# A graph network's last pass: how its row sums and squared deviations are made

## The chip, the cores and the metric

The kernel runs on one core of one Trainium2 chip. A core has TensorE (matrix products), VectorE, ScalarE (functions of one input), GpSimd (general cores, which also issue the indirect transfers), SyncE (which issues plain transfers) and 16 DMA engines between the HBM and its on-chip memory (SBUF, with 128 partitions; TensorE writes to a smaller one, PSUM). The metric is the device time of one execution in microseconds.

## The reference, cut to what matters

Eight layers of a graph network run over 10000 nodes with 512 features and 10000 edges; then the input is added and every row is normalised:

```
for W, b, g, beta in layers:                       # 8
    h = h * norm_out
    agg = segment_sum(h[src], dst) * norm_in
    h = gelu(layer_norm(agg @ W + b, g, beta))
y = x + h
out = (y - mean(y)) / sqrt(var(y) + 1e-5)          # row by row, 512 columns
```

The last two lines are the pass that the change touches.

## The kernel before, in words

After a setup that sorts edges and destinations, each layer gathers rows, sums them with TensorE, multiplies by the layer's weights and normalises. Nodes that receive edges are kept as packed rows; the layer's rows are stored to an HBM table, `h_rows`, and the index `idx_f` says which of its rows belongs to which node.

The last pass goes over 79 tiles of 128 nodes (the last one has 16). The tiles of the input x lie already in `agg_t`, SBUF that the layers no longer need; SyncE loads them beside the last layer. Each engine has its own program, in order, and the engines meet only at semaphores:

- GpSimd issues one indirect transfer per tile (`gather`, L526), which brings the 128 rows of `h_rows` into one of `FS` = 8 row buffers. A gather waits until the addition eight tiles earlier has freed the buffer.
- VectorE adds the buffer onto the tile in place (`add`, L961), takes the batch statistics of the 512 columns (`spread`, L965) and sums them up to mean and variance (`mean`, L969). It runs one addition ahead of the statistics.
- The rest goes by groups of tiles: 1, 1, 2, then groups of 4 (`GROUPS`, 22 in all, the last one of 3). ScalarE adds epsilon to a group's variances (`add_eps`, L1101), GpSimd raises them to the power -1/2 (L537), VectorE makes the shift, minus mean times that (`shift`, L974), and ScalarE scales and shifts each tile in place (`result`, L1107).
- SyncE stores each finished tile (L414).

The order written into the programs matters. GpSimd first issues eight gathers; then, for each group q, it issues the gathers of the tiles eight ahead of it (in the steady part those of group q+2) and behind them the power of group q. VectorE's shift of a group comes `LATE` = 4 tiles after its end (2 for the first groups); the last two shifts come at the very end. ScalarE's order is the epsilon of group q, then the scaling of group q-1. The variances, means and shifts have places for 16 tiles.

Of the kernel before, what the change touches and what calls it, by code (L numbers as in the profile page):

```python
# [6 lines left out]
D = 512  # L7
LAYERS = 8
EPS = 1e-5
P = 128  # L10
# [8 lines left out]
FS = 8  # L19
LATE = 4  # L20
# [16 lines left out]
ALU = mybir.AluOpType  # L37
ACT = mybir.ActivationFunctionType
# [22 lines left out]
def build(nc, x, src, dst, dst_prev, dst_row, Ws, bs, ln_g, ln_b, out):  # L61
# [3 lines left out]
    with ctx:  # L65
# [3 lines left out]
        def sem(n):  # L69
            return ctx.enter_context(nc.semaphore(n))  # L70
# [8 lines left out]
        with nc.sbuf_tensor("rows", [P, UN, D], f32) as gathered:  # L79
            rows = gathered  # L80
# [28 lines left out]
        ps_y = [ctx.enter_context(nc.psum_tensor(f"ps_y{i}", [P, D], f32)) for i in range(2)]  # L109
        ps_z = ctx.enter_context(nc.psum_tensor("ps_z", [P, D], f32))  # L110
        ps_l = [ps_g[:, 2 * i:2 * i + 2, :, :].rearrange("p a k n -> p (a k n)") for i in range(2)]
        ps_f = [ps_g[:, i, :, :].rearrange("p k n -> p (k n)") for i in range(GS)]
# [7 lines left out]
        def view(flat, shape, d):  # L120
            if d is not f32:
                flat = flat.bitcast(d)
            if len(shape) == 3:
                flat = flat.rearrange("p (a b) -> p a b", b=shape[2])
            if len(shape) == 4:
                flat = flat.rearrange("p (a b c) -> p a b c", b=shape[2], c=shape[3])
            if len(shape) == 5:
                flat = flat.rearrange("p (a b c d) -> p a b c d", b=shape[2], c=shape[3], d=shape[4])
            return flat

        def words(shape, d):
            size = 1
            for n in shape[1:]:
                size *= n
            return size * (2 if d is bf16 else 4) // 4

        def part(shape, d=f32):
            n = words(shape, d)
            flat = agg_t[:, :, :].rearrange("p k n -> p (k n)")[0:shape[0], Space.at:Space.at + n]
            Space.at += n  # L140
            return view(flat, shape, d)
# [82 lines left out]

        GX = 4
        Space.at = (GX - 1) * PADDED + (NR // GX - 1) * D
        f_stats, f_mean = part([P, FS, 6]), part([P, 2 * FS, 2])
        f_var, f_rstd, f_shift = part([P, 2 * FS]), part([P, 2 * FS]), part([P, 2 * FS])
        assert GX == KB and Space.at <= KB * PADDED

        def final_rows(t, n):

            at = t // GX * D
            return agg_t[0:n, t % GX, at:at + D]
# [67 lines left out]
        x_in = sem("x_rows_in")  # L302
        hf_in = [sem(f"h_tile_in{k}") for k in range(FS)]
        f_sum = sem("residual_added")
        f_st = sem("final_stats")
        f_mv = sem("final_mean_var")
        f_ve = sem("final_var_eps")
        f_rs = sem("final_rstd")
        f_sh = sem("final_shift")
# [21 lines left out]
        FULL = N // P  # L331
        TAIL = N - FULL * P
        QUADS = NR // GX
        TILES = [(t, P if t < FULL else TAIL) for t in range(FULL + 1)]
        ENDS = [1, 2, 4] + list(range(GX + GX, FULL - 2, GX)) + [FULL - 2, FULL + 1]
        GROUPS = list(zip([0] + ENDS[:-1], ENDS))

        def places(g):

            first = GROUPS[g][0] % (2 * FS)  # L340
            return slice(first, first + GROUPS[g][1] - GROUPS[g][0])
# [200 lines left out]
        def _(dve):  # L542
            v = nc.vector
# [33 lines left out]
            for n, high, low in ((2, dst_hi, dst_lo), (0, src_hi, src_lo)):  # L577
                for c in range(NE // HT):
                    own, packs = slice(c * HT, c * HT + HT), slice(c * HT // G, (c + 1) * HT // G)
# [181 lines left out]
            for c in range(CH):  # L761
                k = c % 2
                if c >= 2:
                    dve.wait_ge(put_ok, c - 1)
                own = slice(c * CT, c * CT + CT)
# [192 lines left out]
            def add(t, n):  # L958
                dve.wait_ge(hf_in[t % FS], 16 * (t // FS + 1))
                own = final_rows(t, n)  # L960
                v.tensor_tensor(own, own, rows[0:n, t % FS, :], ALU.add).then_inc(f_sum, 1)  # L961

            def spread(t, n):
                dve.wait_ge(f_sum, t + 1)
                v.bn_stats(f_stats[0:n, t % FS, :], final_rows(t, n)).then_inc(f_st, 1)  # L965

            def mean(t, n):
                dve.wait_ge(f_st, t + 1)
                v.bn_aggr(f_mean[0:n, t % (2 * FS), :], f_stats[0:n, t % FS, :]).then_inc(f_mv, 1)  # L969

            def shift(q):
                own = places(q)
                dve.wait_ge(f_rs, q + 1)
                v.scalar_tensor_tensor(f_shift[:, own], f_mean[:, own, 0], -1.0, f_rstd[:, own],  # L974
                                       ALU.mult, ALU.mult).then_inc(f_sh, 1)

            dve.wait_ge(x_in, 16 * (QUADS - 1 + FULL % GX + 1))
            add(*TILES[0])
            for t, n in TILES:
                if t < FULL:  # L980
                    add(*TILES[t + 1])
                if t > 0:
                    mean(*TILES[t - 1])
                spread(t, n)
                for q, end in enumerate(ENDS[:-2]):
                    if t == end + (LATE if end > GX else LATE // 2):
                        shift(q)
            mean(*TILES[FULL])
            shift(len(GROUPS) - 2)
            shift(len(GROUPS) - 1)  # L990


        @block.scalar
        def _(act):
            a = nc.scalar
# [27 lines left out]
            for lev in range(LEVELS + 1):  # L1023
                first, end = lev * CH, lev * CH + CH
# [70 lines left out]
                w_stage(L, pairs, its, pb, ib)  # L1095


            def add_eps(q):
                own = places(q)
                act.wait_ge(f_mv, GROUPS[q][1])  # L1100
                a.activation(f_var[:, own], f_mean[:, own, 1], ACT.Copy, bias=EPS).then_inc(f_ve, 1)  # L1101

            def result(q):
                act.wait_ge(f_sh, q + 1)
                for t, n in TILES[GROUPS[q][0]:GROUPS[q][1]]:
                    k, own = t % (2 * FS), final_rows(t, n)
                    a.activation(own, own, ACT.Identity, bias=f_shift[0:n, k:k + 1], scale=f_rstd[0:n, k:k + 1])\  # L1107
                     .then_inc(f_o, 1)

            for q in range(len(GROUPS)):  # L1110
                add_eps(q)
                if q > 0:
                    result(q - 1)
            result(len(GROUPS) - 1)
# [216 lines left out]
```

## Time and profile before

| What | Value |
|---|---|
| median of 3 runs | 1397.96 us (1397.11 to 1398.72) |
| the profiled execution: its span | 1400.9 us |
| the profiled execution: its own time | shown by its span alone, 1400.9 us |
| busy TensorE / VectorE / ScalarE / GpSimd | 1057.1 / 909.9 / 518.2 / 845.7 us |
| the last pass: first gather to the end of the span | 1255.6 to 1400.9 us |
| DMA in the last pass | 41.01 MB, mean 281 GB/s |
| out stores, landing (median) | 4.1 us |

Times in the trace are microseconds from the start of the span. A line such as L526 is a line of the kernel. The profiled execution is one of its own, so a difference is worked out within it and then laid on the median of the runs. An engine's gap is put down to what released it; "issue" is a gap in which it waited for nothing that the profile shows.

### The profile page before, as it was taken

Reading aid. Unit: us, or ns where it says so; the run is one execution under the profiler, and the core shown is the slowest. Engines: PE = TensorE matmul, PEld = TensorE weight load, DVE = VectorE, ACT = ScalarE, POOL = GpSimd, SP = SyncE. Lnnn points to the kernel's source line nnn. Section 1 sums busy time; section 2 is a strip of 40 time slices with the busy share of each in tenths; the row PEclk is TensorE's granted clock in tenths of the full one; section 3 lists DMA queues with packets and bytes.
Section 4 is the critical chain, followed back from the end, with each engine's and each line's share of the span. In section 5 each row is a group of like instructions: output and inputs, shape, how many; then the busy total and the mean of one; then the engine's idle time right before and its main releaser. Section 6 shows DMA issues by size and latency. Waiting matters only on the chain.

```text
span 1400.9 us, 29723 instructions
## 1 busy us (share of the span) xinstructions
PE 1057.1 (75%) x6307; PEld 863.9 (62%) x6307; DVE 909.9 (65%) x2155; ACT 518.2 (37%) x842; POOL 845.7 (60%) x1025
## 2 busy tenths in 40 slices
PE   7896695886968968959968977899688899960000
PEld 7673244776757857857857866788577778840000
DVE  7787895574674764755754774477644377757876
ACT  5324302333324324333334333433244434422545
POOL 1577204566556655655666657667577566658885
PEclk9885597998989989989989999999899999985555
DMA  9700004526336245264265226622466694557998
GB/s 347 270 5 4 2 0 133 153 98 190 119 121 194 85 155 166 82 182 126 90 184 178 85 102 195 186 91 90 142 197 202 183 365 177 176 175 245 322 305 288
DMA packets 98031, 224.47 MB, mean 160 GB/s; under 512 B 14496, under 2 KB 14496, under 8 KB 97968
## 3 DMA queue, kind: packets, MB, share of 16 engines
q0 software_dynamic: 34432, 104.72, 25.7%
q1 hardware_dynamic: 57104, 107.19, 21.4%
q10 hardware_dynamic: 6432, 11.86, 2.3%
q8 instruction: 21, 0.34, 0.1%
q14 instruction: 42, 0.34, 0.1%
HBM read 137.91 MB, written 85.82 MB: 160 GB/s over the span
## 4 chain that ended last, share of the span: by engine, by line
PE 49%; DMA 12%; issue 11%; POOL 9%; DVEq 8%; DVE 8%; ACT 3%; POOLq 0%; ACTq 0%; SPq 0%
PE ps_y L1289 10%; PE ps_y L1294 10%; PE ps_y L1290 10%; DMA rows<-h_rows,slot 7%; PE ps_a L1260 6%; DVEq L863 5%; POOL rows L526 5%; DMA h_rows<-rows 3%; PE ps_y L1285 2%; PE ps_a L1175 2%; PE ps_y L1194 2%; POOL rows L471 2%; PE ps_a L1241 1%; POOL agg_t L537 1%; DMA rows<-h_rows,idx_f 1%
## 5 line engine op out<-in xcount | busy, mean ns | idle before, releaser
L1260 PE MATMUL ps_a<-sel,rows 128*128 128x128 f32 x2560 | 364.3, 293 | 147.4 <-DMA rows<-h_rows,slot 123.2
L1260 PEld LDWEIGHTS ps_a<-sel,rows 128*128 128x128 f32 x2560 | 324.9, 201 | 188.4 <-issue 184.8
L471 POOL DMA_INDIRECT rows<-h_rows,slot x290 | 278.1, 959 | 136.7 <-issue 77.2
L485 POOL TENSOR_TENSOR s_lo<-agg_t,s_hi 128x512 fp32r<-128x512 f32 x168 | 216.9, 1293 | 189.9 <-ACT s_hi L1060 189.9
L1055 ACT ACTIVATE agg_t<-ps_a 128x508 f32 x320 | 190.7, 596 | 348.1 <-PE ps_a L1260 340.9
L830 DVE TENSOR_SCALAR sel<-iota,by_tile 128x128 f32<-128x128 f32 x344 | 136.4, 400 | 227.2 <-issue 227.2
L1289 PE MATMUL ps_y<-w_hi,s_hi 128*128 128x512 f32 x672 | 262.6, 391 | 3.2 <-ACT s_hi L1060 2.8
L1290 PE MATMUL ps_y<-w_lo,s_hi 128*128 128x512 f32 x672 | 261.6, 389 | 0.0
L1294 PE MATMUL ps_y<-w_hi,s_lo 128*128 128x512 f32 x672 | 179.6, 389 | 0.0
L914 DVE BATCH_NORM_STATS2 small<-ps_y 128x6 f32<-128x512 f32 x168 | 117.2, 698 | 63.2 <-PE ps_y L1294 62.4
L1289 PEld LDWEIGHTS ps_y<-w_hi,s_hi 128*128 128x128 f32 x672 | 126.1, 188 | 33.6 <-issue 7.7
L1294 PEld LDWEIGHTS ps_y<-w_hi,s_lo 128*128 128x128 f32 x672 | 126.1, 188 | 26.3
L1290 PEld LDWEIGHTS ps_y<-w_lo,s_hi 128*128 128x128 f32 x672 | 126.1, 188 | 25.8
L1060 ACT ACTIVATE s_hi<-agg_t 128x512 fp32r (+1 forms) x168 | 104.8, 628 | 89.5 <-PE ps_y L1294 42.1
L455 POOL DMA_INDIRECT rows<-out_degrees,agg_t x80 | 79.5, 994 | 62.4 <-DVE agg_t L626 43.2
L493 POOL TENSOR_TENSOR small<-small 128x1 f32<-128x1 f32 x168 | 95.3, 567 | 14.0
L526 POOL DMA_INDIRECT rows<-h_rows,idx_f x79 | 84.1, 1064 | 29.4 <-issue 21.4
L1065 ACT ACTIVATE rows<-ps_a 128x512 f32<-128x512 f32 x84 | 50.3, 599 | 133.6 <-DVE ps_a L929 126.4
L1065 ACT ACTIVATE rows<-ps_z 128x512 f32<-128x512 f32 x84 | 50.4, 600 | 124.9 <-DVE ps_z L929 113.5
L471 POOL DMA_INDIRECT rows<-in_x,slot x30 | 28.8, 958 | 84.2 <-issue 82.0
L961 DVE TENSOR_TENSOR agg_t<-agg_t,rows 128x512 f32<-128x512 f32 (+1 forms) x79 | 54.1, 685 | 32.3 <-DMA rows<-h_rows,idx_f 31.8
L921 DVE SCALAR_TENSOR_TENSOR ps_z<-ps_y,small,rows 128x512 f32<-128x512 f32 x84 | 63.7, 759 | 16.4 <-ACT rows L1065 5.6
(212 smaller groups left out, 1286.5 us busy)
## 6 DMA issues: line engine op xcount, KB each, us to landing
h_rows<-rows SPq DMA_DIRECT2D x124, 256.0 KB, 2.0
h_rows<-agg_t SPq DMA_DIRECT2D x1, 20480.0 KB, 58.6
out<-agg_t SPq DMA_DIRECT2D x78, 256.0 KB, 4.1
agg_t<-in_x SPq DMA_DIRECT2D x19, 1024.0 KB, 5.9
h_rows<-rows ACTq DMA_DIRECT2D x44, 256.0 KB, 2.3
w_raw<-in_Ws SPq DMA_DIRECT2D x32, 256.0 KB, 2.9
rows<-h_rows,slot POOLq DMA_INDIRECT x290, 3.7
rows<-in_ln_g SPq DMA_DIRECT2D x8, 256.0 KB, 3.7
```

Source lines behind the costliest of these rows:

```text
L471: g.indirect_dma_start(out=rows[:, k, :], out_offset=None, in_=table[:, :], in_offset=bass.IndirectOffsetOnAxis(ap=slot[:, k:k + 1], axis=0))\
L485: g.tensor_tensor(s_lo[:, k, :, :], agg_t[:, :, bass.ds(c * P, P)], s_hi[:, k, :, :].bitcast(f32), ALU.subtract).then_inc(lo_ok, 1)
L526: g.indirect_dma_start(out=rows[0:n, t % FS, :], out_offset=None, in_=hbuf[:, :], in_offset=bass.IndirectOffsetOnAxis(ap=idx_f[0:n, t:t + ...
L830: v.tensor_scalar(sel[:, k % GS, :], iota[:, :], rel[:, bass.ds(i, 1)], wgt[:, bass.ds(i, 1)], ALU.is_equal, ALU.mult).then_inc(sel_ok, 1)
L914: v.bn_stats(stats[:, k, :], ps_y[k][:, :]).then_inc(st_ok, 1)
L1055: a.activation(agg_t[:, :, bass.ds(r0 + 1, P - 1)], ps_a[k % GS][:, :, 1:P], ACT.Copy)\
L1060: a.activation(s_hi[:, k, :, :], agg_t[:, :, bass.ds(c * P, P)], ACT.Copy).then_inc(hi_ok, 1)
L1065: a.activation(made[k], ps_t[k], ACT.Gelu).then_inc(h_ok, 1)
L1260: m = mm(ps_a[k % GS][:, b, :], rows[:, k, b * P:(b + 1) * P], sel[:, k % GS, :], start=True, stop=True)
L1289: mm(ps_y[k][:, :], s_hi[:, k, b, :], w_hi[:, b, :], start=False, stop=False)
L1290: mm(ps_y[k][:, :], s_hi[:, k, b, :], w_lo[:, b, :], start=False, stop=False)
L1294: m = mm(ps_y[k][:, :], s_lo[:, k, b, :], w_hi[:, b, :], start=False, stop=b == KB - 1)
```

## The change: row sums from the addition, squares from ScalarE

The addition also gives the sum of each row. VectorE turns a group's sums into negated means. ScalarE computes the square of each tile with that negated mean as bias, writes the squares to PSUM (they are not used again) and keeps their sum; VectorE turns a group's sums into variance plus epsilon. The batch statistics and ScalarE's epsilon go. VectorE's program now goes by groups: the additions of group q, with the variance of group q-2 behind the first of them, then the mean of q and the shift of q-2. ScalarE's order is the squares of q, then the scaling of q-1. GpSimd's program is as it was.

```diff
             def add(t, n):
                 dve.wait_ge(hf_in[t % FS], 16 * (t // FS + 1))
                 own = final_rows(t, n)
-                v.tensor_tensor(own, own, rows[0:n, t % FS, :], ALU.add).then_inc(f_sum, 1)
+                v.scalar_tensor_tensor(own, own, 1.0, rows[0:n, t % FS, :], ALU.mult, ALU.add,
+                                       accum_out=f_total[0:n, t % (2 * FS):t % (2 * FS) + 1]).then_inc(f_sum, 1)
+
+            def mean(q):
+                own = places(q)
+                dve.wait_ge(f_sum, GROUPS[q][1])
+                v.tensor_scalar(f_negm[:, own], f_total[:, own], -1.0 / D, None, ALU.mult).then_inc(f_nm, 1)
+
+            def variance(q):
+                own = places(q)
+                dve.wait_ge(f_sq, GROUPS[q][1])
+                v.tensor_scalar(f_var[:, own], f_square[:, own], 1.0 / D, EPS, ALU.mult, ALU.add).then_inc(f_ve, 1)
...
-            add(*TILES[0])
-            for t, n in TILES:
-                if t < FULL:
-                    add(*TILES[t + 1])
-                if t > 0:
-                    mean(*TILES[t - 1])
-                spread(t, n)
-                for q, end in enumerate(ENDS[:-2]):
-                    if t == end + (LATE if end > GX else LATE // 2):
-                        shift(q)
-            mean(*TILES[FULL])
-            shift(len(GROUPS) - 2)
-            shift(len(GROUPS) - 1)
+            for q, (first, last) in enumerate(GROUPS):
+                for t, n in TILES[first:last]:
+                    add(t, n)
+                    if t == first and q > 1:
+                        variance(q - 2)
+                mean(q)
+                if q > 1:
+                    shift(q - 2)
+            for q in (len(GROUPS) - 2, len(GROUPS) - 1):
+                variance(q)
+                shift(q)
...
+            def squares(q):
+                act.wait_ge(f_nm, q + 1)
+                for t, n in TILES[GROUPS[q][0]:GROUPS[q][1]]:
+                    k = t % (2 * FS)
+                    if t >= len(f_seen):
+                        act.wait_ge(f_sq, t - len(f_seen) + 1)
+                    a.activation(f_seen[t % len(f_seen)][0:n, :], final_rows(t, n), ACT.Square,
+                                 bias=f_negm[0:n, k:k + 1], accum_out=f_square[0:n, k:k + 1]).then_inc(f_sq, 1)
...
             for q in range(len(GROUPS)):
-                add_eps(q)
+                squares(q)
                 if q > 0:
                     result(q - 1)
             result(len(GROUPS) - 1)
```

`f_seen` is seven PSUM tiles that the layers no longer need. The shift keeps its place in the chain and multiplies the negated mean by the power.

## Rows read from the trace of the kernel before

**Rows 1.** Stretches of the pass: us, busy us of each engine, clock, DMA share, GB/s

```profile
core 0 of [0], span 1400.9 us
...
1260.00:1280.00 20.00, 0.00 (x0) 0.00 (x0) 13.87 (x34) 3.74 (x8) 16.36 (x16) 0.50 0.67 187
1280.00:1300.00 20.00, 0.00 (x0) 0.00 (x0) 16.60 (x43) 9.40 (x15) 16.58 (x17) 0.50 0.92 311
...
1340.00:1360.00 20.00, 0.00 (x0) 0.00 (x0) 15.74 (x40) 9.40 (x15) 16.62 (x16) 0.50 0.92 312
```

**Rows 2.** Chain of waits from 1220 us to the end, shares by line

```profile
by line: POOL rows L526 39.0%; issue 12.4%; POOL agg_t L537 9.9%; DMA rows<-h_rows,idx_f 9.4%; PE ps_y L1294 4.4%; PE ps_y L1289 4.0%; PE ps_y L1290 4.0%; ACT agg_t L1107 4.0%; DMA h_rows<-rows 3.3%; DVE agg_t L961 2.5%; DVE agg_t L965 1.6%
```

**Rows 3.** Groups of instructions, 1255 to 1401 us: busy us, mean ns | idle before

```profile
L526 POOL DMA_INDIRECT rows<-h_rows,idx_f x79 | 84.1, 1064 | 29.4 <-issue 21.4 <-DMA h_rows<-rows 6.2 <-DVE agg_t L961 1.7
L1107 ACT ACTIVATE agg_t<-agg_t 128x512 f32<-128x512 f32 x78 | 57.2, 802 | 12.6 <-DVE agg_t L974 12.6
L961 DVE TENSOR_TENSOR agg_t<-agg_t,rows 128x512 f32<-128x512 f32 x78 | 53.4, 685 | 32.3 <-DMA rows<-h_rows,idx_f 31.8
L965 DVE BATCH_NORM_STATS2 agg_t<-agg_t 128x6 f32<-128x512 f32 x78 | 51.4, 659 | 0.0
L537 POOL TENSOR_TENSOR agg_t<-agg_t,small 128x4 f32<-128x4 f32 x18 | 21.8, 1210 | 3.5 <-ACT agg_t L1101 3.1
L969 DVE BATCH_NORM_AGGREGATE agg_t<-agg_t 128x2 f32<-128x6 f32 x78 | 13.5, 173 | 0.0
L1101 ACT ACTIVATE agg_t<-agg_t 128x4 f32<-128x4 f32 x18 | 3.7, 205 | 57.2 <-DVE agg_t L969 57.2
L974 DVE SCALAR_TENSOR_TENSOR agg_t<-agg_t 128x4 f32<-128x4 f32 x18 | 2.6, 142 | 0.0
```

**Rows 4.** Order of instructions on VectorE and GpSimd: start us, us, engine, line

```profile
1316.30 0.69 DVE L961 TENSOR_TENSOR agg_t<-agg_t,rows 128x512 f32<-128x512 f32 x1 [0.61 <-DMA rows<-h_rows,idx_f]
...
1316.42 1.39 POOL L526 DMA_INDIRECT rows<-h_rows,idx_f  x1 [0.30 <-issue]
...
1318.11 0.95 POOL L526 DMA_INDIRECT rows<-h_rows,idx_f  x1 [0.30 <-issue]
...
1320.68 1.05 POOL L526 DMA_INDIRECT rows<-h_rows,idx_f  x1 [0.19 <-issue]
```

**Rows 5.** Waits from 1255 us on: engine line, waited for, us, times, longest

```profile
POOL rows L526 <- DVE agg_t L961: 1.7, 6, 0.3
```

**Rows 6.** Gathers: time to landing over the pass; tile 56, then tile 72, with additions

```profile
DMA to landing us min/median/max: 3.3/5.1/6.7
...
1347.73 1.41 POOL L526 DMA_INDIRECT rows<-h_rows,idx_f  x1 [0.19 <-issue]
...
1352.51 0.69 DVE L961 TENSOR_TENSOR agg_t<-agg_t,rows 128x512 f32<-128x512 f32 x1 [0.40 <-DMA rows<-h_rows,idx_f]
...
1374.95 1.07 POOL L526 DMA_INDIRECT rows<-h_rows,idx_f  x1 [0.19 <-issue]
...
1378.91 0.67 DVE L961 TENSOR_TENSOR agg_t<-agg_t,rows 128x512 f32<-128x512 f32 x1
```

**Rows 7.** The end: addition of tile 75, last shift of four, the scalings

```profile
1384.91 0.74 DVE L961 TENSOR_TENSOR agg_t<-agg_t,rows 128x512 f32<-128x512 f32 x1 [0.49 <-DMA rows<-h_rows,idx_f]
...
1389.26 0.14 DVE L974 SCALAR_TENSOR_TENSOR agg_t<-agg_t 128x4 f32<-128x4 f32 x1
...
1389.44 2.93 ACT L1107 ACTIVATE agg_t<-agg_t 128x512 f32<-128x512 f32 x4 [0.44 <-DVE agg_t L974]
...
1396.59 0.80 ACT L1107 ACTIVATE agg_t<-agg_t 16x512 f32<-16x512 f32 x1
```

**Rows 8.** The page's groups: Gelu without pointer, three-operand form with PSUM input

```profile
L1065 ACT ACTIVATE rows<-ps_a 128x512 f32<-128x512 f32 x84 | 50.3, 599 | 133.6 <-DVE ps_a L929 126.4
...
L921 DVE SCALAR_TENSOR_TENSOR ps_z<-ps_y,small,rows 128x512 f32<-128x512 f32 x84 | 63.7, 759 | 16.4 <-ACT rows L1065 5.6
```

More of the change, by code:

```diff
@@ L226, in build @@
         Space.at = (GX - 1) * PADDED + (NR // GX - 1) * D
-        f_stats, f_mean = part([P, FS, 6]), part([P, 2 * FS, 2])
+        f_total, f_negm, f_square = part([P, 2 * FS]), part([P, 2 * FS]), part([P, 2 * FS])
         f_var, f_rstd, f_shift = part([P, 2 * FS]), part([P, 2 * FS]), part([P, 2 * FS])
+        f_seen = [ps_y[0][:, :], ps_y[1][:, :]] + ps_f
         assert GX == KB and Space.at <= KB * PADDED
@@ L304, in build @@
         f_sum = sem("residual_added")
-        f_st = sem("final_stats")
-        f_mv = sem("final_mean_var")
+        f_nm = sem("final_negated_mean")
+        f_sq = sem("final_squares_summed")
         f_ve = sem("final_var_eps")
@@ L960, in add @@
                 own = final_rows(t, n)
-                v.tensor_tensor(own, own, rows[0:n, t % FS, :], ALU.add).then_inc(f_sum, 1)
[L963 to L969, printed above, removed]
+                v.scalar_tensor_tensor(own, own, 1.0, rows[0:n, t % FS, :], ALU.mult, ALU.add,
[8 more added lines that the diff above has]
+                v.tensor_scalar(f_var[:, own], f_square[:, own], 1.0 / D, EPS, ALU.mult, ALU.add).then_inc(f_ve, 1)
             def shift(q):
@@ L973, in shift @@
                 dve.wait_ge(f_rs, q + 1)
-                v.scalar_tensor_tensor(f_shift[:, own], f_mean[:, own, 0], -1.0, f_rstd[:, own],
-                                       ALU.mult, ALU.mult).then_inc(f_sh, 1)
+                v.tensor_tensor(f_shift[:, own], f_negm[:, own], f_rstd[:, own], ALU.mult).then_inc(f_sh, 1)
             dve.wait_ge(x_in, 16 * (QUADS - 1 + FULL % GX + 1))
-            add(*TILES[0])
-            for t, n in TILES:
-                if t < FULL:
-                    add(*TILES[t + 1])
-                if t > 0:
-                    mean(*TILES[t - 1])
-                spread(t, n)
-                for q, end in enumerate(ENDS[:-2]):
-                    if t == end + (LATE if end > GX else LATE // 2):
-                        shift(q)
-            mean(*TILES[FULL])
-            shift(len(GROUPS) - 2)
-            shift(len(GROUPS) - 1)
+            for q, (first, last) in enumerate(GROUPS):
[9 more added lines that the diff above has]
+                shift(q)
         @block.scalar
@@ L1095, in _ @@
                 w_stage(L, pairs, its, pb, ib)
[L1098 to L1101, printed above, removed]
+            def squares(q):
[6 more added lines that the diff above has]
+                                 bias=f_negm[0:n, k:k + 1], accum_out=f_square[0:n, k:k + 1]).then_inc(f_sq, 1)
             def result(q):
```

## The prediction

> **What bounds the kernel now.** I read the stretch table first, then the chain of waits, then the groups of instructions by line, then the order of GpSimd's and VectorE's instructions, and last the end of the run. From 1260 us TensorE has no instruction left, while the 16 DMA engines are 0.92 busy in both later stretches shown and GpSimd is busy for 16.4 to 16.6 us of every 20 [rows 1]. Everything the diff touches lies in this last pass, some 145 us, so only it is to be priced. In the chain the largest share is GpSimd's gathers at L526 (39.0%), then its issue gaps, its power function at L537 (9.9%) and the landing of gathers (9.4%); VectorE's addition and statistics have 2.5% and 1.6%, ScalarE's scaling 4.0% [rows 2]. So the pass goes at the pace of GpSimd: per group of four tiles it issues four gathers and one power, back to back. Four gathers of a mean 1.064 us [rows 3] with three gaps of 0.30 [rows 4] make 5.16 us from the first gather to the power; with the power's 1.21 [rows 3] and 0.19 of gap behind it [rows 4] a group takes 6.6 us. The DMA engines are close behind; VectorE and ScalarE have room: per tile VectorE holds 0.685 + 0.659 + 0.173 us and ScalarE 0.80 [rows 3] of 1.65.
>
> **Taken out.** Per tile the 0.659 us statistics and the 0.173 us that sum them up, and per group ScalarE's 0.205 us copy with the epsilon [rows 3]. None is on GpSimd's path in the steady part: GpSimd waited for an addition only 1.7 us in all, six times [rows 5]. I book 1.0 us of that as saved; between 0 and 1.7 is possible.
>
> **Put in, VectorE.** The addition becomes a three-operand instruction with a sum. No such instruction with both large inputs in SBUF is in the trace; the bounds are the plain addition, 0.685 [rows 3], and the three-operand form with an input in PSUM, 0.759 [rows 8]. I take 0.76, and 0.10 for reading the sum out, between nothing and the 0.173 of the smallest statistics instruction [rows 3]: 0.86 (0.685 to 0.93, and one dear case among the rivals). Three small instructions per group at about 0.15, like the shift of 0.142 [rows 3], change nothing by their length: VectorE is at 4 x 0.86 + 0.45 = 3.9 us of a 6.6 us group.
>
> **Put in, ScalarE.** One square per tile with one pointer operand. The scaling with two pointers takes 0.80 and starts every 0.71 (four in 2.93) [rows 3, 7], the Gelu without a pointer 0.60 [rows 8]. Midway, less the same overlap, is 0.61; with a read-out that costs up to the 0.205 of a tiny instruction I take 0.80 (ends 0.51, the 0.60 less the overlap, and 1.0, the 0.80 plus 0.205). ScalarE then needs 4 x 0.71 + 4 x 0.80 + 0.3 of starting = 6.3 us per group: it just fits into 6.6, and becomes the bound when a square costs over about 0.9.
>
> **The wait that moves: GpSimd.** Before, the power of a group needs the statistics of its own last tile, which are there 1 to 2 additions after that tile has landed; GpSimd was never held by it in the steady part (its idle time before the four-column powers is 3.5 us in 18, 3.1 of it waiting for ScalarE at the very end) [rows 3]. After, the variance of group q-2 is computed by VectorE behind the first addition of group q. In program order GpSimd issues the four gathers of group q and then that power. So the power now needs the first of the four gathers just issued to have landed, and the next four gathers are queued behind the power. The eight row buffers no longer help: one landing stands in every turn. From landing to the power I count 0.76 + 0.10 + 0.15 for the variance and 0.14 for three hand-overs (a scaling started 0.04 behind the end of its shift, 1389.26 + 0.14 to 1389.44 [rows 7]; I allow 0.05 each) = 1.15. GpSimd comes to the power 5.16 after the first gather. It stalls by (landing + 1.15 - 5.16), so from a landing time of 4.0 us on. Over the pass a landing takes 3.3 to 6.7, median 5.1; of first gathers of a group, tile 56 took 4.8 (1347.73 to its waiting addition at 1352.51), tile 72 at most 4.0 (1374.95 to 1378.91) [rows 6]. They come after GpSimd's pause, so they are below the median, and the pause grows: a stall empties the DMA engines, which are 0.92 busy now. I take 4.4, between these two: 0.4 per group. The turns that delay later gathers are groups 3 to 18, 16 of them: 6.4 us (0 at a landing of 4.0 or less; 16 x 1.1 = 18 at the median of all).
>
> Behind VectorE's new waits stand the other additions of group q; eight gathers ahead wait for those, which is far. Squares of a group end about 0.3 + 2.8 + 3.2 = 6.3 us after its mean, and their variance is asked for a group and a first addition (about 9 us) after it: that wait is hidden, and stays so until a square costs about 1.4.
>
> **The end.** Before, ScalarE ran 11 scalings from 1389.44, the last ending at 1397.39, and the span ends 3.5 us later [rows 1, 7]. After, result(18) can start only behind mean(20), which follows the addition of tile 75 (1384.91 [rows 7]): with 0.86, the mean, the shift and hand-overs, at 1386.2. From there ScalarE's queue is without a gap: 15 scalings x 0.71 and seven squares x 0.80 (groups 20 and 21) = 16.2 us, to 1402.4. That is 5.0 us later than before, and nothing hides it, since the stores follow the scalings (3.0 with squares of 0.51, 6.4 with 1.0). The chains variance-power-shift of groups 20 and 21 (about 2 us each) lie beside scalings.
>
> **Sum.** 5.0 + 6.4 - 1.0 = +10.4 us. The profiled execution has a span of 1400.9 [rows 1]; the median shown is 1397.96, 2.9 below it, so I take the difference over unchanged: 1408.4 us.
>
> **A rule against it.** A gather that starts inside an addition is held until the addition is over: the one at 1316.42, 0.12 behind the start of an addition, ran 1.39, the one at 1318.11, where an addition was about to end, 0.95 [rows 4]. Mean 1.064 against 0.95 is 0.11 per gather. So the length of the addition counts on GpSimd too. The Trainium skill (Vector Engine (DVE) Microarchitecture Reference, Points that are easy to get wrong) says that the scalar-tensor-tensor shape with two non-bf16 sources in SBUF halves its throughput, having no port left to read the accumulator back. By that 512 more cycles, an estimate of 0.53 us per addition, would come on top, some 8 us over 16 releases before any blocking. No run here shows it yet.
>
> **The rivals.**
> (a) No stall: first landings stay at or under 4.0 because the pause in gathers drains the engines. For it: tile 72. Against: tile 56. Then only the end pays: 1398 + 5.0 - 1.0 = 1402.
> (b) The summing addition is dear: it costs a pass for the addition and another for the sum, 0.685 + 0.659 = 1.34 [rows 3]. For it: no two-input summing form is in the trace. Against: the PSUM form at 0.759. Each release comes 0.5 later, +8 over 16 groups; and the blocking of gathers, 0.11 now, grows with the square of the length, to about 0.4. Since it is partly absorbed by the stall, I add half of 64 x 0.3 = 19, some 9: 1425.
> (c) ScalarE becomes the bound: a square of 1.0 makes 7.1 us per group against 7.0 with the stall: +2, and the end +1.4: 1412. Over that it decides.
> (d) The other side, not slower: VectorE is idle more, additions start at the landing and not from a backlog, and fall clear of the gathers' starts. The 0.11 per gather goes, 79 x 0.11 = 8.7 us [rows 3, 4]. It needs landings under 4.0, and decides from 4.0 us on, 0.05 per gather. All of it gives 1402 - 8.7 = 1393, half of it 1397.6. Against: an addition that waits for landings starts at any phase, so 0.11 may as well grow.
>
> **How the numbers follow.** Forecast 0.47 (its own range 1404 to 1416); (a) 0.18; (b) 0.13; (c) 0.05; (d) 0.17, of which 0.08 are faster by over 0.2% (2.8 us, what a measurement can tell from no change) and 0.09 within it. With 0.01 of (a) falling inside, slower has 0.82, the same 0.10, faster 0.08. The range 1398 to 1424 leaves out most of (d) and half of (b).
>
> **What would show it.** Right: GpSimd idle before most four-column powers, released by VectorE's variance, 0.2 to 0.8 each; an addition at 0.76 and a square starting every 0.7 to 0.9; ScalarE gapless over the last 16 us; the last scaling some 5 us farther behind the last addition. Wrong: powers without idle time (a), additions over 1.2 us (b), ScalarE without any wait for shifts throughout (c), gathers at 0.95 throughout (d).

## The result and the profile after

The changed kernel takes 1415.95 us (1413.31 to 1418.14) against 1398.34 of the kernel before; the ratio is 1.0122, interval 1.0101 to 1.0142: some 17 us slower. On another chip, beside its variants, the same kernel gave 1.0105 (1.0070 to 1.0140).

First the stretches of the last pass, as in [rows 1]; line numbers in the changed kernel are one to five higher than before.

```profile
core 0 of [0], span 1416.0 us
...
1280.00:1300.00 20.00, 0.00 (x0) 0.00 (x0) 7.86 (x28) 15.66 (x33) 15.10 (x15) 0.50 0.87 272
...
1340.00:1360.00 20.00, 0.00 (x0) 0.00 (x0) 6.98 (x26) 12.88 (x28) 14.12 (x14) 0.50 0.85 271
...
1400.00:1416.00 16.00, 0.00 (x0) 0.00 (x0) 0.67 (x4) 12.25 (x25) 1.86 (x2) 0.50 0.52 193
```

GpSimd, busy 16.6 us in every 20 before, is busy 14.1 to 15.1 now, and the DMA engines 0.85 to 0.87 instead of 0.92. VectorE fell to half (16.60 and 15.74 to 7.86 and 6.98), ScalarE rose. The chain over the pass has a new head, the landings of gathers: 42.3% against 11.7% before. ([rows 2] begin at 1220 us, which is why they have 9.4%.) First the pass of the kernel before, then that of the changed kernel:

```profile
by line: POOL rows L526 48.5%; issue 14.5%; POOL agg_t L537 12.4%; DMA rows<-h_rows,idx_f 11.7%; ACT agg_t L1107 4.9%; DVE agg_t L961 3.1%; DVE agg_t L965 2.0%; ACTq L65 0.5%; DVE agg_t L969 0.3%; ACT agg_t L1101 0.1%; DVE agg_t L974 0.0%
...
by line: DMA rows<-h_rows,idx_f 42.3%; POOL rows L527 18.7%; POOL agg_t L538 11.0%; issue 8.6%; DVE agg_t L962 7.2%; ACT agg_t L1112 5.8%; ACT ps_a L1105 2.1%; ACT ps_y L1105 0.9%; DVE agg_t L973 0.6%; ACTq L65 0.4%; DVE agg_t L978 0.1%; DV
```

The groups of instructions, to be held against [rows 3]:

```profile
L527 POOL DMA_INDIRECT rows<-h_rows,idx_f x78 | 82.6, 1059 | 23.2 <-issue 21.4 <-DVE agg_t L962 1.8
L962 DVE SCALAR_TENSOR_TENSOR agg_t<-agg_t,rows 128x512 f32<-128x512 f32 x78 | 53.6, 692 | 86.6 <-DMA rows<-h_rows,idx_f 86.5
L1105 ACT ACTIVATE ps_a<-agg_t 128x512 f32<-128x512 f32 x55 | 36.9, 671 | 0.0
L538 POOL TENSOR_TENSOR agg_t<-agg_t,small 128x4 f32<-128x4 f32 x18 | 21.1, 1175 | 19.5 <-DVE agg_t L973 19.3
...
L1105 ACT ACTIVATION_READ_ACCUMULATOR ps_a<-agg_t 128x1 f32 x55 | 10.3, 186 | 0.0
L962 DVE DVE_READ_ACCUMULATOR agg_t<-agg_t,rows 128x1 f32 x78 | 6.5, 83 | 0.0
```

Each sum is read out by an instruction of its own, 0.083 us on VectorE and 0.186 on ScalarE. The addition is at 0.692 against 0.685, the gathers at 1.06 as before. What is new is the idle time ahead of the powers at L538: 19.5 us, 19.3 of it released by VectorE's variance at L973. The waits say the same (engine and line, waited for, us, times, longest), and show [rows 5] unchanged in their last line:

```profile
DVE agg_t L962 <- DMA rows<-h_rows,idx_f: 86.5, 62, 9.3
...
POOL agg_t L538 <- DVE agg_t L973: 23.2, 13, 3.9
...
POOL rows L527 <- DVE agg_t L962: 1.8, 7, 0.3
```

Of the 23.2 us, 9.3 lie in the last three powers (below); the other 13.9 are in groups 3 to 18 and hold up gathers. Two turns, one slow and one fast, in the order of time (start us, us, engine, line, idle before):

```profile
1334.54 2.91 ACT L1112 ACTIVATE agg_t<-agg_t 128x512 f32<-128x512 f32 x4
...
1339.21 1.01 POOL L527 DMA_INDIRECT rows<-h_rows,idx_f  x1 [0.19 <-DVE agg_t L962]
...
1342.19 2.93 ACT L1112 ACTIVATE agg_t<-agg_t 128x512 f32<-128x512 f32 x4 [1.92 <-DVE agg_t L978]
...
1345.24 0.69 DVE L962 SCALAR_TENSOR_TENSOR agg_t<-agg_t,rows 128x512 f32<-128x512 f32 x1 [3.08 <-DMA rows<-h_rows,idx_f]
...
1345.86 0.17 DVE L973 TENSOR_SCALAR agg_t<-agg_t 128x4 f32<-128x4 f32 x1
1345.93 0.69 DVE L962 SCALAR_TENSOR_TENSOR agg_t<-agg_t,rows 128x512 f32<-128x512 f32 x1
1346.11 1.41 POOL L538 TENSOR_TENSOR agg_t<-agg_t,small 128x4 f32<-128x4 f32 x1 [2.13 <-DVE agg_t L973]
...
1347.71 1.02 POOL L527 DMA_INDIRECT rows<-h_rows,idx_f  x1 [0.19 <-issue]
...
1351.35 0.69 DVE L962 SCALAR_TENSOR_TENSOR agg_t<-agg_t,rows 128x512 f32<-128x512 f32 x1 [2.02 <-DMA rows<-h_rows,idx_f]
...
1352.90 1.04 POOL L538 TENSOR_TENSOR agg_t<-agg_t,small 128x4 f32<-128x4 f32 x1
...
1354.13 1.01 POOL L527 DMA_INDIRECT rows<-h_rows,idx_f  x1 [0.19 <-issue]
```

In the first turn the gather of 1339.21 is added at 1345.24, 6.03 later; the power, 0.87 behind that, ran 1.41, beginning inside the next addition (1345.93); the turn took 8.50 us. In the second the addition came after 3.64, the power found its variance ready, and the turn took 6.42. Ahead of the slow one ScalarE's four scalings, each followed by a store, ended at 1337.45; ahead of the fast one at 1345.12, 2.6 us before the gather. Over the pass the turns took 7.44 us (tile 12 at 1273.60 to tile 76 at 1392.65, 16 turns) against 6.59 before (1275.68 to 1381.05): 13.6 us. The rest of the loss lies behind the last gather. There the span goes on for 20.6 us (1395.38 to 1416.0) against 16.9 (1383.99 to 1400.9), 3.7 more. The gathers outside these turns take 0.4 less, so the whole pass, from the first gather, takes 162.2 against 145.3 us, +16.9.

The end, to be held against [rows 7]:

```profile
1396.64 2.93 ACT L1112 ACTIVATE agg_t<-agg_t 128x512 f32<-128x512 f32 x4 [3.01 <-DVE agg_t L978]
...
1398.27 1.03 POOL L538 TENSOR_TENSOR agg_t<-agg_t,small 128x4 f32<-128x4 f32 x1 [2.02 <-DVE agg_t L973]
...
1399.48 0.67 ACT L1105 ACTIVATE ps_a<-agg_t 128x512 f32<-128x512 f32 x1
...
1402.30 2.91 ACT L1112 ACTIVATE agg_t<-agg_t 128x512 f32<-128x512 f32 x4
...
1402.67 1.01 POOL L538 TENSOR_TENSOR agg_t<-agg_t,small 128x4 f32<-128x4 f32 x1 [3.36 <-DVE agg_t L973]
...
1405.11 0.67 ACT L1105 ACTIVATE ps_a<-agg_t 128x512 f32<-128x512 f32 x1
...
1407.22 5.02 ACT L1112 ACTIVATE agg_t<-agg_t 128x512 f32<-128x512 f32 x7
...
1407.60 0.85 POOL L538 TENSOR_TENSOR agg_t<-agg_t,small 128x3 f32<-128x3 f32 x1 [3.92 <-DVE agg_t L973]
```

ScalarE works without a gap from 1396.64 to 1412.24: four scalings, four squares, four scalings, three squares, seven scalings. A square starts every 0.70 us.

### The profile page after: what moved, and what is told of

Same layout as the page of the kernel before. It is cut to its first block, busy times and chain, and to the rows that moved or that the text cites. A ratio compares the mean times of both kernels' runs of the same rounds, so it can differ in the third digit from the quotient of the medians.

```text
span 1416.0 us, 29842 instructions
## 1 busy us (share of the span) xinstructions
PE 1056.2 (75%) x6307; PEld 864.2 (61%) x6307; DVE 865.1 (61%) x2120; ACT 569.0 (40%) x978; POOL 844.3 (60%) x1025
## 4 chain that ended last, share of the span: by engine, by line
PE 48%; DMA 16%; issue 10%; DVE 8%; DVEq 8%; POOL 6%; ACT 3%; POOLq 0%; ACTq 0%; SPq 0%
PE ps_y L1294 10%; PE ps_y L1295 10%; PE ps_y L1299 10%; DMA rows<-h_rows,slot 7%; PE ps_a L1265 6%; DVEq L864 5%; DMA rows<-h_rows,idx_f 5%; DMA h_rows<-rows 3%; PE ps_y L1290 2%; POOL rows L527 2%; POOL rows L472 2%; PE ps_a L1180 2%; PE ps_y L1199 2%; PE ps_a L1246 1%; POOL agg_t L538 1%
## 5 line engine op out<-in xcount | busy, mean ns | idle before, releaser
L962 DVE SCALAR_TENSOR_TENSOR agg_t<-agg_t,rows 128x512 f32<-128x512 f32 (+1 forms) x79 | 54.2, 692 | 86.6 <-DMA rows<-h_rows,idx_f 86.5
L922 DVE SCALAR_TENSOR_TENSOR ps_z<-ps_y,small,rows 128x512 f32<-128x512 f32 x84 | 63.7, 759 | 16.2 <-ACT rows L1066 5.4
```

## The experiments

**The wait alone.** In the kernel before, GpSimd also waits for the first addition two groups on; nothing of the change is in it.

```diff
                 pool.wait_ge(f_ve, q + 1)
+                if 2 < q < len(GROUPS) - 2:
+                    pool.wait_ge(f_sum, GROUPS[q + 2][0] + 1)
```

> The kernel before, with one wait more: GpSimd waits, ahead of the power of group q (groups 3 to 19), until the first addition of group q+2 is made. Nothing else is changed. Theory (the wait alone makes the steady loss): 10 to 14 us slower than before, groups at 7.2 to 7.5 us instead of 6.6, GpSimd idle before the powers for some 15 us in all, first landings of a group at 5 us or more. Rival (the new instructions make it, by their length or by blocking GpSimd): within 2 us of before.

Measured: 1.0042 (1.0023 to 1.0062), +6 us: neither. Its powers (shown further below) wait 12.9 us in all, of which 8.9 lie between the fourth gather's end and the power in groups 3 to 18, and they last 1.03 instead of 1.21, which gives 3 us back. A turn takes 6.84. So the wait is a cause by itself, and something in the changed kernel makes it twice as dear.

**The sum alone.** In the kernel before, only the addition takes the summing form.

```diff
-                v.tensor_tensor(own, own, rows[0:n, t % FS, :], ALU.add).then_inc(f_sum, 1)
+                v.scalar_tensor_tensor(own, own, 1.0, rows[0:n, t % FS, :], ALU.mult, ALU.add,
+                                       accum_out=f_total[0:n, t % (2 * FS):t % (2 * FS) + 1]).then_inc(f_sum, 1)
```

> The kernel before, with the addition in the summing three-operand form and nothing else new: batch statistics stay, the sums are not used. Theory: the form costs 0.08 us of VectorE per tile, which no one waits for: within 2 us of before. Rival (the summing addition is dear or blocks GpSimd's gathers longer): 6 us slower or more, gathers at a mean of 1.15 us or more instead of 1.06.

Measured: 0.9992 (0.9973 to 1.0012), no change; the addition at 0.685 and the gathers at 1.043 us. The dear addition falls.

**The powers two gathers later**, in the changed kernel:

```diff
+            sent = FS
             for q, (first, last) in enumerate(GROUPS):
-                for t, n in TILES[first + FS:last + FS]:
+                for t, n in TILES[sent:max(sent, last + FS + (2 if q > 2 else 0))]:
                     gather(t, n)
+                sent = max(sent, last + FS + (2 if q > 2 else 0))
```

> The changed kernel, with GpSimd's power of each group from the fourth on placed two gathers later in its program. Theory (the wait): the landing that the power needs has then 2.7 us more and the stall goes; groups back to 6.5 to 6.7 us, what is left is the end: 3 to 5 us slower than before, 12 to 14 faster than the changed kernel. Rival (ScalarE's squares or VectorE's new order make the loss): still 14 us or more slower than before.

Measured: 1.0031 (1.0010 to 1.0052), +4 us, with every new instruction in place. The powers' idle time falls from 19.5 to 5.1 us, all but 0.4 of it in the end, and a turn takes 6.50. What is left is the end: ScalarE's last scaling ends 11.7 us behind the last addition (1387.62 to 1399.36), 7.4 before (1389.99 to 1397.39).

```profile
L540 POOL TENSOR_TENSOR agg_t<-agg_t,small 128x4 f32<-128x4 f32 x18 | 21.7, 1206 | 5.1 <-DVE agg_t L975 4.7
```

**Half the stores.** The left 256 columns of each tile are stored, the rest is left out.

```diff
-                sp.dma_start(out[t * P:t * P + n, :], final_rows(t, n)).then_inc(o_st, 16)
+                sp.dma_start(out[t * P:t * P + n, 0:D // 2], final_rows(t, n)[:, 0:D // 2]).then_inc(o_st, 16)
```

> The changed kernel storing only the left 256 of the 512 columns of each output tile; the rest of the output is left out. It asks why the landings stayed long although GpSimd paused. Theory (a burst of four stores lies in front of each group's gathers): first landings fall from about 5.2 to 4.2 us or less, GpSimd's wait before the powers from 16 us to under 5, and the kernel is 8 to 14 us faster than the changed one. Rival (the gathers themselves take that long): first landings stay at 5 us or more and the time within 4 us of the changed kernel's but for a shorter last store.

Measured: 1.0053 (1.0035 to 1.0071), against 1.0105 of the changed kernel on another chip: some 7 to 10 us less. From gather to addition the first of a group takes 4.28 on average, at most 5.0 (the changed kernel 4.95, at most 6.24), and GpSimd's stall in groups 3 to 18 falls from 14.1 to 6.1 us, where under 5 was expected; a turn takes 6.85. The stores do lengthen the landings; since the DMA engines have less to do in all, this alone doesn't say that their place does.

**The shift early.** VectorE makes the shift of group q-2 right behind its variance, so it stands still while the power runs, and ScalarE scales earlier.

```diff
                     if t == first and q > 1:
                         variance(q - 2)
+                        if q > 4:
+                            shift(q - 2)
                 mean(q)
-                if q > 1:
+                if 1 < q <= 4:
                     shift(q - 2)
```

> The changed kernel with VectorE's shift of group q-2 moved (from group 3 on) from behind the mean of group q to right behind the variance of q-2, so that VectorE waits there for the power, and ScalarE scales, and SyncE stores, some 2.5 us earlier in each turn. GpSimd's program and its wait for the first addition stay. Theory (the wait costs what it does because four stores are issued just in front of the gathers, and because the next addition blocks the power): first landings go back to 3.6 to 4.5 us in nearly all groups, powers last 1.04 instead of up to 1.41, GpSimd waits under 6 us in the steady part instead of 16, groups take 6.4 to 6.7 us, and the end is 2 to 3 us shorter as well: 10 to 15 us faster than the changed kernel, 1 to 6 slower than before. Rival (any wait for a landing in GpSimd's turn costs this): within 4 us of the changed kernel, since the wait is still there.

Measured: 1.0071 (1.0049 to 1.0094), +10 us, less of a gain than expected. The powers are all at 1.03 to 1.05, and first landings are over 5.0 us in four groups of 16 instead of nine, but they average 4.72 and not 4.0; the stall is 7.6 us. A turn takes 6.91. The scalings, and behind them the stores, no longer end ahead of the first gather: in ten of the 16 groups the next four scalings begin as it does, so the stores run beside the gathers. One of the ten:

```profile
1336.22 1.01 POOL L527 DMA_INDIRECT rows<-h_rows,idx_f  x1 [0.19 <-issue]
1336.26 2.93 ACT L1114 ACTIVATE agg_t<-agg_t 128x512 f32<-128x512 f32 x4 [0.83 <-DVE agg_t L978]
```

**The shift early, the scaling held back** until the mean of group q, as in the changed kernel:

```diff
             def result(q):
                 act.wait_ge(f_sh, q + 1)
+                if 2 < q < len(GROUPS) - 2:
+                    act.wait_ge(f_nm, q + 3)
```

> The kernel with the early shift, but ScalarE holds the scaling of group q-2 until the mean of group q is there, as in the changed kernel; so VectorE still stands still while the power runs, and the stores go out as late as in the changed kernel. It tells apart what the early shift gained. Theory (the place of the store burst in front of the gathers): first landings alternate again between 3.6 and 6 us, powers stay at 1.04, and of the early shift's gain only the shorter powers (seven or eight times 0.37, 3 us) is left: 11 to 15 us slower than before. Rival (the blocked power, or VectorE's order, was all of it): as with the early shift, 8 to 11 us slower.

Measured: 1.0114 (1.0084 to 1.0144), some 16 us and as slow as the changed kernel beside it (1.0105). So the gain of the early shift came from the earlier scalings and stores; the shorter powers alone gave nothing. The groups of the three kernels (wait alone, early shift, early shift with the scaling held):

```profile
L539 POOL TENSOR_TENSOR agg_t<-agg_t,small 128x4 f32<-128x4 f32 x18 | 18.6, 1033 | 12.9 <-DVE agg_t L963 12.4 <-ACT agg_t L1103 0.5
```

```profile
L527 POOL DMA_INDIRECT rows<-h_rows,idx_f x79 | 84.5, 1070 | 29.4 <-issue 19.0 <-DMA h_rows<-rows 6.2 <-DVE agg_t L962 4.1
L538 POOL TENSOR_TENSOR agg_t<-agg_t,small 128x4 f32<-128x4 f32 x18 | 18.6, 1034 | 12.4 <-DVE agg_t L973 12.1
```

```profile
L527 POOL DMA_INDIRECT rows<-h_rows,idx_f x79 | 88.5, 1120 | 29.9 <-issue 20.8 <-DMA h_rows<-rows 6.7 <-DVE agg_t L962 2.3
L538 POOL TENSOR_TENSOR agg_t<-agg_t,small 128x4 f32<-128x4 f32 x18 | 18.6, 1034 | 17.2 <-DVE agg_t L973 17.1
```

Held back, the four scalings end 0.6 to 1.7 us ahead of the first gather in 12 of the 16 groups, as in the changed kernel; first landings are over 5.0 us in 12, and the stall is back to 11.2 us. Of the difference of 0.48 us per turn (7.39 to 6.91) 0.22 is stall and 0.26 longer gathers, which go to 1.12. More of them begin inside an addition, but the hold is not shown to be why: with the early shift and the end by statistics (below), where nothing is held back, they are at 1.09.

**The changed kernel again**, without an edit, for the comparison on that chip.

> The changed kernel as it is, on the same chip as its variants, to have their differences in one place: 15 to 19 us slower than before.

Measured: 1.0105 (1.0070 to 1.0140), 14.7 us, a shade under the expectation. Its trace shows how much one execution differs from the next: a turn takes 7.25 and not 7.44, the stall is 13.1 and not 14.1, and the pass takes 158.7 us, 13.4 more than before and not 16.9.

**The end by statistics.** The powers two later as above, and the last two groups (seven tiles) go through batch statistics on VectorE, which give the negated mean and the variance; ScalarE squares nothing there. Of the edit, ScalarE's part:

```diff
...
             for q in range(len(GROUPS)):
-                squares(q)
+                if q < len(GROUPS) - 2:
+                    squares(q)
```

> The changed kernel with the powers two gathers later, as measured, and the last two groups (seven tiles) done by VectorE's batch statistics instead of ScalarE's squares. Theory (the end is ScalarE's queue without a gap, and a square starts every 0.70): 7 x 0.70 = 4.9 us less than with the powers two later alone: within 2 us of before. Rival (the end is set by the stores): the same as with the powers two later alone, about 4 us slower than before.

Measured: 0.9996 (0.9983 to 1.0010), equal to before. The powers two later alone were at 1.0031 on another chip, 4.9 us more, give or take 3.5. In the traces the stretch from the last gather's start to the end falls from 20.1 to 17.3 us (before: 16.9), so of the 3.2 us added there 2.8 are gone with the seven squares; the turns took 6.40 instead of 6.50, another 1.6 us, which this experiment does not explain. ScalarE's last eleven scalings follow each other in one row:

```profile
1388.95 7.86 ACT L1143 ACTIVATE agg_t<-agg_t 128x512 f32<-128x512 f32 x11 [2.41 <-DVE agg_t L1000]
```

**Both, with the powers in place**: the early shift and the end by statistics.

> Both together without moving the powers: the shift right behind the variance, and the last two groups by batch statistics. If both theories hold, 2 to 4 us faster than with the early shift alone, since part of the end is gained by either: from 2 us faster to 2 us slower than before. If the wait for a landing is what costs, still 8 us or more slower than before.

Measured: 1.0044 (1.0029 to 1.0058), 3.8 us under the early shift alone. That is the size expected of the end, but the traces do not show it there: the pass takes 150.3 us against 151.3, since the early shift alone had already brought the stretch behind the last gather's start to 17.9 (now 17.1), and the rest of the difference between these two executions lies ahead of the pass, where the kernels are the same. Against before neither outcome came, since the early shift cures half the stall only.

**The power off GpSimd, kernel before.** ScalarE takes the root, VectorE the reciprocal; GpSimd only issues gathers.

```diff
-                own = places(q)
-                pool.wait_ge(f_ve, q + 1)
-                g.tensor_tensor(f_rstd[:, own], f_var[:, own], mhalf[:, :].to_broadcast([P, own.stop - own.start]),
-                                ALU.pow).then_inc(f_rs, 1)
...
                 own = places(q)
+                dve.wait_ge(f_ve, q + 1)
+                v.reciprocal(f_rstd[:, own], f_var[:, own]).then_inc(f_rs, 1)
                 dve.wait_ge(f_rs, q + 1)
...
-                a.activation(f_var[:, own], f_mean[:, own, 1], ACT.Copy, bias=EPS).then_inc(f_ve, 1)
+                a.activation(f_var[:, own], f_mean[:, own, 1], ACT.Copy, bias=EPS).then_inc(f_ep, 1)
+                act.wait_ge(f_ep, q + 1)
+                a.activation(f_var[:, own], f_var[:, own], ACT.Sqrt).then_inc(f_ve, 1)
```

> The kernel before with the power taken off GpSimd: ScalarE takes the square root of variance plus epsilon, VectorE the reciprocal ahead of the shift. It asks whether GpSimd's turn (6.6 us, of it 1.4 for the power) or the DMA engines (busy 0.92 to 0.95) set the pace. Theory (GpSimd): groups at 5.5 us until the DMA engines are full at about 6.2: 5 to 8 us faster than before. Rival (the DMA engines set it already): within 2 us of before.

Measured: 0.9962 (0.9943 to 0.9980), 5.3 us faster than before, the fastest of all. GpSimd's turn is 5.50, and the DMA engines are then full:

```profile
1290.00:1370.00 80.00, 0.00 (x0) 0.00 (x0) 74.42 (x192) 46.34 (x82) 55.78 (x52) 0.50 0.98 328
```

0.98 busy at 328 GB/s. The gathers run ahead (their median landing goes from 5.1 to 7.2) and the pass is paced by the DMA engines, which is why 17 us of gain in issuing became 5.

**The power off GpSimd, changed kernel**, with ScalarE's root ahead of its scaling; VectorE's and GpSimd's parts are as above but for the semaphore that VectorE waits for:

```diff
...
             def result(q):
+                act.wait_ge(f_ve, q + 1)
+                a.activation(f_var[:, places(q)], f_var[:, places(q)], ACT.Sqrt).then_inc(f_ro, 1)
                 act.wait_ge(f_sh, q + 1)
```

> The changed kernel with the power taken off GpSimd: ScalarE takes the root of a group's variances just ahead of its scaling, VectorE the reciprocal ahead of the shift. GpSimd then only issues gathers and waits for no landing. Theory (the wait in GpSimd's turn is the whole steady loss): the steady part is as fast as in the kernel before with its power off GpSimd, and only the end (4 to 5 us of squares) is left between the two: 2 us faster to 2 slower than before. Rival (the squares or the late results cost by themselves): 6 us or more slower than before.

Measured: 0.9980 (0.9965 to 0.9995), 2.8 us faster than before and about 19 better than the changed kernel by their medians (1397.51, 1416.24). The squares and the new order of VectorE are all in it; GpSimd's wait is not, but neither is the power itself, so the 19 us are not the wait's alone. The like comparison is with the kernel before without its power (0.9962): there the change costs some 2.5 us instead of 15 to 17. And the steady part has a new bound. The additions of tiles 48 and 52 begin 6.28 us apart, ScalarE is busy 18.67 of every 20 us from 1290 to 1370, and VectorE waits 48.1 us in all for its roots:

```profile
1330.00:1350.00 20.00, 0.00 (x0) 0.00 (x0) 9.09 (x36) 18.67 (x42) 13.03 (x14) 0.50 1.03 326
...
DVE agg_t L975 <- ACT agg_t L1109: 48.1, 17, 5.1
...
1333.20 0.68 DVE L959 SCALAR_TENSOR_TENSOR agg_t<-agg_t,rows 128x512 f32<-128x512 f32 x1
...
1339.48 0.69 DVE L959 SCALAR_TENSOR_TENSOR agg_t<-agg_t,rows 128x512 f32<-128x512 f32 x1
1339.60 2.93 ACT L1113 ACTIVATE agg_t<-agg_t 128x512 f32<-128x512 f32 x4 [0.45 <-DVE agg_t L977]
```

ScalarE's four squares, root and four scalings, with 0.45 us between root and scaling, set the pace here: rival (c), once GpSimd no longer waits. The DMA engines are full as well (1.00 to 1.03 over these stretches, in which a packet counts whole where it starts), but the first gathers of groups have then landed mostly some 4 us before their additions begin.

## Why the prediction came out as it did

The forecast was +10.4 us and slower with 0.82; measured were +17.6 by the medians, within the range of 1398 to 1424 and at the very end of the forecast's own, 1404 to 1416. By its steps:

- **The wait that moves** was right as a mechanism. GpSimd is idle before ten of the 16 powers of groups 3 to 18, released by VectorE's variance (0.7 to 2.1 us each, not 0.2 to 0.8); placing the powers two gathers later brings the turn back to 6.50 us, taking GpSimd out of it makes the changed kernel faster than before.
- **Its size was the term that failed**: 6.4 us forecast, 13.6 measured in the turns. The step was "a stall empties the DMA engines", from which I took first landings of 4.4 us. As a reading of the kernel before that was fair: there the same 16 gathers land after 4.55 on average (3.7 to 5.5). In the changed kernel they got slower, 4.93. From gather to addition they averaged 4.95 and came in two kinds: nine over 5.0, up to 6.2, the others down to 3.6. From landing to power it is 0.87, not 1.15, so a stall begins at 4.3; the mean alone would give 0.65 per turn, 10.4 us, but a fast landing gives nothing back, and the stall is 14.1. What held the landings up is, at least in part, where the stores fall. The late shift lets ScalarE scale four tiles in a row, with a store behind each, and in ten groups these scalings end 0.4 to 1.9 us ahead of the next first gather, which then took 5.45 on average (4.1 to 6.2); in five groups with 2.0 us or more it took 3.8, and in the last one, where the scalings ended 0.3 behind the gather's start, 5.6. Holding the scalings back or letting them go (1.0114 to 1.0071) shows that their place is a cause; halving the stores shows from the other side that the stores are. The wait in the old order of VectorE and ScalarE costs 6 us, near the 6.4 of the forecast by coincidence: its stall is 8.9, and powers shortened by 3 us, which the forecast did not have, give the rest back. Why the early shift leaves first landings at 4.72 is not settled: in most groups the stores then run beside the first gathers, and no run separates this from the gathers' own time.
- **The end**: 5.0 forecast. From the shift of group 18 to the last scaling 16.2 us were forecast and 15.6 came; a square was 0.70, not 0.80. The last scaling ends 12.6 us behind the last addition, 5.2 more than before. In the total it shows as 3.7, since the last addition begins 3.6 us behind its gather's start and not 5.3. Its cause is shown: without the seven squares the stretch behind the last gather's start is within 0.4 us of before.
- **Saved waits of GpSimd for additions**, booked at 1.0: nothing (1.7 to 1.8 us).
- **Costs at nothing** held: the sum in the addition costs no time (0.9992), and the squares of the steady part cost none either as long as GpSimd issues the powers (6.50 us per turn with the powers two later, 6.59 before).
- **Rival (b), the dear addition**, falls. The addition with two inputs from SBUF and a sum takes 0.692 us, not 1.34. The Trainium skill (Vector Engine (DVE) Microarchitecture Reference, Points that are easy to get wrong) says that this form with two inputs from SBUF that are not bf16 runs at half its throughput. That is not borne out here: the plain addition of the same tiles takes 0.685, and the read-out 0.083. (a) falls, since ten of 16 turns stall; (d) falls, since the gathers stay at 1.06; (c) does not arise at 0.70 per square, but does once the power is off GpSimd.

The blocking of GpSimd by additions was there, but the change did not add to it: gathers stayed at 1.06, and powers that begin inside an addition ran 1.40 instead of 1.03, as such powers also did before (up to 1.52), so that their mean fell from 1.21 to 1.18. With the wait alone in the kernel before, the power begins behind the addition, beside a one-input statistics instruction, and all powers are at 1.03 to 1.04. The Trainium skill (SBUF — State Buffer, Who interferes with whom) says that a VectorE instruction with two inputs from SBUF contends with a GpSimd instruction that reads SBUF, while one with at most one such input, outside the two-port modes, does not. These rows agree. They also show that it matters which begins first: an addition that began 0.43 us into such a power took its 0.68, and the power 1.04.

## What to carry to other kernels

Before moving work between engines, ask for each in-order queue what its next instruction will wait for, and whether the thing waited for was issued by the same queue just before: that turns a latency that eight buffers had hidden into part of every turn. A latency that is read from a trace holds for that trace's order of transfers; a change that delays a producer also bunches the transfers behind it, so bound such a term by the slow end of what the trace shows, and remember that early arrivals don't pay for late ones. And where a queue sets the pace, its own small instruction is the first thing to move: the root on two engines with room gave what no change to the sums could.

## What the runs showed that I had not expected

Gathers alone do not fill the DMA engines. The DMA view of the changed kernel's slow turn, first from 1339 to 1340 us, with stores (q1) beside gathers (q0), then from 1342.2 to 1344.6, with three to four gathers under way and no store:

```profile
DMA packets 184, 0.41 MB, mean 412 GB/s; under 512 B 22, under 2 KB 22, under 8 KB 184
...
q1 hardware_dynamic: 144, 0.25, 65.8%
q0 software_dynamic: 40, 0.16, 38.9%
...
DMA packets 129, 0.42 MB, mean 176 GB/s; under 512 B 26, under 2 KB 26, under 8 KB 129
...
q0 software_dynamic: 129, 0.42, 76.2%
```

It is 412 GB/s together and 176 for gathers by themselves. So stores and gathers that alternate, instead of running side by side, lose throughput, and in this turn they alternate. It is not this turn alone. From tile 12's gather to tile 76's, cut into slices of 0.5 us, gathers have the DMA engines to themselves (stores busy under 0.03, gathers over 0.1) in 79 of 239 slices of the changed kernel and 33 of 211 of the kernel before, and move 190 GB/s there in either. And VectorE's and ScalarE's sums cost a read-out instruction of 0.083 and 0.186 us, both small enough to hide in the steady part.
